# A graph network on one core: first edges of visits by plain transfers, stagings on SyncE, and 14 scatters moved ahead of a run of gathers

## The reference

```
h = relu(layernorm(x))
x = x + gcn(relu(gcn(h)))            # gcn(h) = D^-1/2 (A + I) D^-1/2 h W + b
h = relu(layernorm(x))
msg = relu([h[src], attr] @ W1 + b1)             # one message for each edge
agg = segment_sum(msg, dst) / max(count(dst), 1)
x = x + relu([h, agg] @ W2 + b2)
```

## Time and profile before

| | us |
|---|---|
| median of 3 runs | 2456.9 (2456.45 to 2467.43) |
| the profiled execution, own time | 2462.0 |
| its span | 2460.1 |
| POOL busy | 1822.6 (74%) |
| PE busy | 2155.0 (88%) |
| DVE busy | 1870.1 (76%) |
| ACT busy | 1241.6 (50%) |

### The profile page before, as it was taken

The page is one execution under the profiler, slowest core; times in us unless marked ns, Lnnn a source line. Parts: engine busy times, 40 slices in busy tenths (PEclk is TensorE's granted clock), DMA queues, the critical chain, the costliest instruction groups (busy, mean ns, idle before and its releaser), DMA issues.

```text
span 2460.1 us, 45677 instructions
## 1 busy us (share of the span) xinstructions
PE 2155.0 (88%) x15568; PEld 1771.9 (72%) x15569; DVE 1870.1 (76%) x3574; ACT 1241.6 (50%) x3349; POOL 1822.6 (74%) x1687
## 2 busy tenths in 40 slices
PE   0344899999999998799995599999999999999996
PEld 0133679997667897688884487887787878888885
DVE  6999999998889884544447377777777777777777
ACT  5846246665666773555557243444444434444440
POOL 0867877888888787777777777777777777777770
PEclk9867999999999998999998799999999999999999
DMA  9414233333334351588874243434434343434432
GB/s 359 173 39 140 74 127 127 135 126 126 124 124 163 141 188 45 166 325 302 322 282 149 70 145 103 142 109 121 131 106 145 106 141 109 131 120 118 133 86 60
DMA packets 127247, 358.89 MB, mean 146 GB/s; under 512 B 34082, under 2 KB 77831, under 8 KB 117687
## 3 DMA queue, kind: packets, MB, share of 16 engines
q10 hardware_dynamic: 24752, 186.56, 19.9%
q0 software_dynamic: 56880, 85.25, 13.5%
q1 hardware_dynamic: 45369, 84.00, 9.9%
HBM read 229.75 MB, written 125.93 MB: 145 GB/s over the span
## 4 chain that ended last, share of the span: by engine, by line
PE 52%; POOL 17%; DVE 15%; issue 8%; ACT 4%; DMA 3%; DVEq 1%; POOLq 0%; ACTq 0%; SPq 0%
POOL rows L803 14%; PE ps_feat L1102 6%; PE ps_node L1102 6%; PE ps_node L1117 5%; PE ps_feat L1117 5%; DVE region_c L2079 5%; PE ps_sum L1212 3%; ACT rows L1318 3%; PE pre_banks L1090 3%; PE ps_extra L1250 3%; POOL permuted L821 2%; PE pre_banks L1203 2%; PE ps_feat L1234 2%; PE ps_node L1234 2%; PE ps_sum L1234 2%
## 5 line engine op out<-in xcount | busy, mean ns | idle before, releaser
L821 POOL DMA_INDIRECT permuted<-rows_or_lows,slot_of_edge x768 | 902.5, 1175 | 234.0 <-issue 151.7
L803 POOL DMA_INDIRECT rows<-table,region_a x800 | 786.1, 983 | 243.8 <-issue 236.8
L2079 DVE TENSOR_TENSOR region_c<-iota_key,region_c 128x1568 bf16<-128x1568 f16 (+1 forms) x327 | 355.8, 1088 | 0.0
L1435 ACT ACTIVATE region_a<-pre_banks 128x392 bf16<-128x392 f32 x392 | 195.0, 499 | 146.3 <-PE pre_banks L1090 138.3
L1102 PE MATMUL ps_node<-region_a,region_b 128*128 128x256 bf16 (+1 forms) x1911 | 263.8, 268 | 4.1 <-issue 4.1
L1102 PE MATMUL ps_feat<-region_a,region_b 128*128 128x256 bf16 x1764 | 252.5, 272 | 0.0
L584 DVE CAST wide_counts<-region_a 128x1024 fp32r<-128x1024 bf16 (+2 forms) x163 | 117.2, 723 | 156.4 <-PE ps_node L1117 69.1
L1250 PE MATMUL ps_extra<-msg_parts,target_hot 128*128 128x256 f32 x1176 | 222.7, 305 | 13.8 <-DVE msg_parts L2264 13.6
L582 ACT ACTIVATE wide_counts<-region_a 128x1024 fp32r<-128x1024 bf16 x150 | 158.6, 1060 | 120.7 <-PE ps_node L1117 56.9
L2279 DVE TENSOR_TENSOR target_hot<-consts,region_a 128x512 fp32r<-128x512 f32 x336 | 207.5, 618 | 1.0
L1212 PE MATMUL ps_sum<-onehot,rows 128*128 128x64 f32 x1600 | 202.3, 270 | 0.0
(11 more groups left out here) (319 smaller groups left out, 4790.0 us busy)
## 6 DMA issues: line engine op xcount, KB each, us to landing
counts<-region_a ACTq DMA_DIRECT2D x23, 3136.0 KB
region_a<-counts ACTq DMA_DIRECT2D x11, 3200.0 KB
region_a<-counts ACTq DMA_DIRECT2D x11, 3072.0 KB
rows_or_lows<-block_lows ACTq DMA_DIRECT2D x72, 448.0 KB
permuted<-region_b SPq DMA_DIRECT2D x25, 833.0 KB, 24.4
region_a<-permuted SPq DMA_DIRECT2D x24, 833.0 KB
rows_or_lows<-edge_cols_in POOLq DMA_DIRECT2D x24, 544.0 KB
region_a<-attr_t_in SPq DMA_DIRECT2D x50, 256.0 KB, 2.8
```

Source lines behind the costliest of these rows:

```text
L803: nc.gpsimd.indirect_dma_start(rows[:, s, j * D:(j + 1) * D], None, tables[2], bass.IndirectOffsetOnAxis(ap=message_rows[:, c * TC + j:c * ...
L821: nc.gpsimd.indirect_dma_start(permuted, bass.IndirectOffsetOnAxis(ap=slot_of_edge[:, r * RT + k:r * RT + k + 1], axis=0), edge_rows_of[:, ...
L1435: nc.scalar.activation(counts[strip % 2][:, :, j * W:j * W + W], count_banks[w % BANKS][:, 0:KEYS].rearrange("p (d h) -> p h d", h=SB), AC ...
L2079: v.tensor_tensor(hot_key(u)[:, :, 0:n], iota_key[:, None, 0:n].to_broadcast([P, UNIT // SIDE, n, SIDE]), keys[:, :, None, :].to_broadcast ...
```

## The change

It has four parts.

1. The 21 gathers of starts leave GpSimd. In their place 19 plain transfers (`START_RUNS`) copy from `starts_dram` to a new DRAM array `visit_starts_dram`: a run takes n nodes that lie a fixed step apart and repeats each k times, 4 bytes at a time. SyncE issues ten of them, ScalarE nine, and they copy 2,688 elements (the longest run has 452 x 2). When all have landed SyncE reads the array back into `visit_starts_i` (21 x 128).
2. `find_visits` leaves node phase 0. VectorE waits for that read ahead of node phase 0, shifts and converts the starts, TensorE turns them, and VectorE adds `visit_plan`. TensorE waits for the starts ahead of its first products of node phase 0.
3. GpSimd does 14 scatters of range 0 ahead of its wait for `visit_rows_ready`, and the wait for `blanked` comes before them.
4. SyncE stages ranges 2 to 13, after `store_own(0)`, each when range r-2 has landed; GpSimd stages 0, 1 and 14 to 23.

To keep the number of semaphores, `late_blocks` becomes a `link` (VectorE waits for its own instruction at once) and `late_scanned` is counted on `rank_hot`.

```diff
+def runs_of(parts):
+    runs, visit = [], 0
+    for target, k in parts:
+        if runs and runs[-1][3] == k and (runs[-1][2] == 1 or target - runs[-1][1] == runs[-1][2] * runs[-1][4]):
+            first, at, n, _, step = runs[-1]
+            runs[-1] = (first, at, n + 1, k, step if n > 1 else target - at)
+        else:
+            runs.append((visit, target, 1, k, W))
+        visit += k
+    return runs
+START_RUNS = runs_of(VISIT_TARGETS + [(0, VB * P - sum(VISITS))])
...
+        def spread_starts(engine, run):
+            visit, target, n, k, step = run
+            of = starts_dram[target:target + n * step].rearrange("(n w) a -> n w a", w=step)[:, 0:1].to_broadcast([n, k, 1])
+            engine.dma_start(visit_starts_dram[visit:visit + n * k].rearrange("(n k) a -> n k a", k=k), of,
+                             allow_slow_non_contiguous=True).then_inc(starts_gathered, 16)
+        def stage(engine, r):
+            if r >= 2:
+                engine.wait_ge(scattered[r % 2], (r // 2) * RT * 16)
+            engine.dma_start(edge_rows_of[:, r % 2], ...)
...
 SyncE, behind the read of ends_i:
+            sp.wait_ge(starts_moved, 16)
+            for run in START_RUNS[0::2]:
+                spread_starts(sp, run)
+            sp.wait_ge(starts_gathered, 16 * len(START_RUNS))
+            sp.dma_start(visit_starts_i, visit_starts_dram.rearrange("(b p) a -> b (p a)", p=P)).then_inc(starts_gathered, 16)
 SyncE, behind store_own(0):
+                    for r in range(2, STAGED_BY_SP):
+                        stage(sp, r)
...
 GpSimd:
-            pool.wait_ge(starts_moved, 16)
-            for b in range(VB):
-                nc.gpsimd.indirect_dma_start(visit_start[:, b:b + 1], None, starts_dram, ...).then_inc(starts_gathered, 16)
-            pool.wait_ge(visit_rows_ready, 1)
+            pool.wait_ge(blanked, 16 * (RANGES + 1))
+            scatter(0, end=AHEAD_OF_VISITS)
+            pool.wait_ge(visit_rows_ready, 3)
...
 TensorE, ahead of node phase 0:
+            pe.wait_ge(visit_rows_ready, 1)
+            nc.tensor.transpose(ps_sum[0][:, 0:VB], visit_starts, ident[0:VB, 0:VB]).then_inc(visit_rows_ready, 1)
             pe.wait_ge(rank_taken, EARLY * len(BLOCK_GROUPS))
...
 ScalarE, ahead of its wait for degree_ready:
+            act.wait_ge(starts_moved, 16)
+            for run in START_RUNS[1::2]:
+                spread_starts(act, run)
...
 VectorE:
             ranks_taken(EARLY - 1)
+            dve.wait_ge(starts_gathered, 16 * len(START_RUNS) + 16)
+            link(v.tensor_single_scalar(visit_starts_i, visit_starts_i, 4, ALU.arith_shift_right))
+            v.tensor_copy(visit_starts, visit_starts_i).then_inc(visit_rows_ready, 1)
             (count copied from TensorE's bank)
+            dve.wait_ge(visit_rows_ready, 2)
+            v.tensor_tensor(visit_row[:], ps_sum[0][:, 0:VB], visit_plan[:], ALU.add).then_inc(visit_rows_ready, 1)
...
-                        if n == 0 and g == VISIT_ROWS_AT:
-                            find_visits()
```

More of the change, by code:

```diff
@@ L101 @@
 FIRST_LOWS_AT = (4, 7, 9)
+STAGED_BY_SP = 14
+AHEAD_OF_VISITS = 14
 KEYS = W * SB
@@ L157, in build @@
         tiles_dram = nc.dram_tensor("tiles", (2, NT), I32, kind="Internal").ap()
+        visit_starts_dram = nc.dram_tensor("starts_of_visits", (VB * P, 1), I32, kind="Internal").ap()
         starts_dram = nc.dram_tensor("starts_of_nodes", (NP, 1), I32, kind="Internal").ap()
@@ L240, in build @@
         visit_key_kept = carve(VB)
+        visit_starts_i = carve(P, I32)[0:VB]
+        visit_starts = carve(P)[0:VB]
         used[0] = 0
@@ L437, in build @@
         late_loaded = sem("late_loaded")
-        late_blocks = sem("late_blocks")
-        late_scanned = sem("late_scanned")
+        rows_staged_by_sp = [sem("rows_staged_by_sp_0"), sem("rows_staged_by_sp_1")]
         rows_staged = [sem("rows_staged_0"), sem("rows_staged_1")]
@@ L806, in gather_messages, with scatter @@
                         ).then_inc(e["gathered"][s], 16)
-            def stage(r):
-                pool.dma_start(edge_rows_of[:, r % 2], t["edge_cols"][:, r * RT:(r + 1) * RT].rearrange("p t c -> p (t c)")
-                               ).then_inc(rows_staged[r % 2], 16)
-            def scatter(r, pace=lambda k: None):
+            def scatter(r, pace=lambda k: None, first=0, end=RT):
                 pool.wait_ge(ranked, r + 1)
-                pool.wait_ge(rows_staged[r % 2], 16 * (r // 2 + 1))
-                for k in range(RT):
-                    if k == RT // 2 and 1 <= r < RANGES - 1:
-                        pool.wait_ge(scattered[(r - 1) % 2], ((r - 1) // 2 + 1) * RT * 16)
-                        stage(r + 1)
+                staged(pool, r)
+                for k in range(first, end):
+                    if k == RT // 2 and STAGED_BY_SP <= r + 1 < RANGES:
+                        stage(pool, r + 1)
                     pace(k)
@@ L838, in beside_phase @@
                 pool.wait_ge(G["tab"], group(n, i * NG // (PHASED[n] * RT)) + 1)
-            stage(0)
-            stage(1)
+            stage(pool, 0)
+            stage(pool, 1)
             pool.wait_ge(loaded, 16 * N_LOADS)
@@ L876, in _ @@
                 for r in range(PHASED[n]):
-                    scatter(next(ranges), lambda k: beside_phase(n, r * RT + k))
+                    scatter(next(ranges), lambda k: beside_phase(n, r * RT + k), first=0 if n else AHEAD_OF_VISITS)
                 if n == 0:
@@ L1877, in _ @@
             link(v.reciprocal(degree[:], degree[:]))
-            def find_visits():
-                dve.wait_ge(starts_gathered, 16 * VB)
-                link(v.tensor_single_scalar(visit_start[:], visit_start[:], 4, ALU.arith_shift_right))
-                v.tensor_tensor(visit_row[:], visit_start[:], visit_plan[:, 1], ALU.add).then_inc(visit_rows_ready, 1)
             def scales_of(g):
@@ L2370 @@
     at = ROW * np.arange(EDGE_ROWS)[:, None] + np.arange(P)[None, :]
-    visit_of = np.zeros((3, VB * P), np.int32)
-    parts_of = [(w * W + j * (W // len(splits)), k) for w, splits in zip(WINDOW_AT, SPLITS) for j, k in enumerate(splits)]
-    target_of = np.concatenate([np.full(k, target) for target, k in parts_of])
-    visit_of[0, :sum(VISITS)] = target_of
-    visit_of[1, :sum(VISITS)] = np.concatenate([np.arange(k) for _, k in parts_of]) * (P // ROW)
-    visit_of[2, :sum(VISITS)] = -target_of * SB
-    visit_of = visit_of.reshape(3, VB, P).transpose(2, 0, 1)
+    visit_of = np.zeros((2, VB * P), np.int32)
+    visit_of[0, :sum(VISITS)] = np.concatenate([np.arange(k) for _, k in VISIT_TARGETS]) * (P // ROW)
+    visit_of[1, :sum(VISITS)] = -SB * np.concatenate([np.full(k, target) for target, k in VISIT_TARGETS])
+    visit_of = visit_of.reshape(2, VB, P).transpose(2, 0, 1)
     node_half = P * np.arange(SB)[None, :] + np.arange(P)[:, None] - 0.5
```

27 lines of the change are left out of this document (14 added, 13 removed).

## The result

The changed kernel takes 2475.97 us (median, 2474.68 to 2478.5), the kernel before 2458.18 us beside it on the same chip (2456.45 to 2467.43). The ratio is 1.0066, with a 95% interval of 1.0044 to 1.0089: **slower by 0.7%**, 17.8 us by the medians. The forecast was 2441.1 us. The profiled execution took 2475.01 us; its span is 2473.1, 13.0 us over that of before.

What follows compares the result with a forecast made beforehand. POOL was taken to bound the kernel; -17.3 us (its lateness at the messages) + 1.5 (path) + 0 (stall) = -15.8 us, taking the median from 2456.9 to 2441.1 us. Range 2436 to 2468, the forecast's own 2436 to 2445.

Steps and rivals of the forecast that it cites:

- Stall: 0: At VectorE's new wait ahead of node phase 0: starts back at about 162 to 163, so no stall.
- the starts come so late that the kernel is slower: Rival at VectorE's wait ahead of node phase 0: slower from a stall of 28 us; chance 0.14.
- The elements: In the 19 small transfers: the longest run, 904 elements on one engine at 11.9 ns, takes 10.8 us.
- The rest of the chain: Issues of 0.31 to 0.36 us, last out at about 152; landing about 1.4 us, the read back once more.
- the 3 us to spare: At VectorE's new wait: starts back at about 162 to 163, 3 us spare before any stall.
- POOL's lateness, 17.3 us: At the first gather of messages: POOL starts at 1371.09, the table landed at 1353.8; at most 17.3 us to win.
- The end of the table: Before the messages: the last table transfer, issued at 1351.5, lands 2.3 us later.
- The messages move as a whole: Messages and output groups move with the first chunk, for which VectorE, TensorE and ScalarE stand idle.
- The added path, 1.5 us: On VectorE's path from 166.05 through node phase 0: the added work costs 1.5 us together.
- The 14 scatters: In POOL's idle time from 136.98: 20.7 us, up to 7.5 more beside scans, ending between 158 and 165.
- Part 4, 7 to 11 us: In POOL's scatters: 12 stagings moved to SyncE save 0.6 to 0.9 us each, 7 to 11 us.
- the first gather of messages at about 1355: Sign of a right forecast: POOL's first gather of messages at about 1355 us, after waiting for the last table transfer.

Runs made afterwards that it cites:

- e7: The changed kernel with long runs cut evenly (27 transfers) and the transfers with most elements issued first; 2451.75 us, ratio 0.9966 to the kernel before.
- e10: The changed kernel with GpSimd staging all ranges again, the 14 early scatters kept; 2471.71 us, ratio 1.0046 to the kernel before.
- e8: The changed kernel with GpSimd staging all ranges again and no scatters ahead of the visit edges; 2483.27 us, ratio 1.0079 to the kernel before.
- e1: The changed kernel with every long run cut so its main part is a multiple of 16 (27 transfers); 2455.08 us, ratio 0.998 to the kernel before.
- e9: e6 with ScalarE's first load_lows held until the last table is stored; 2446.22 us, ratio 0.9937 to the kernel before.
- e4: The kernel before with only the stagings of ranges 2 to 13 moved to SyncE, plus small edits; 2458.71 us, ratio 0.999 to the kernel before.
- e5: The kernel before with the small edits and 14 more plain transfers on POOL that nobody reads; 2475.87 us, ratio 1.0063 to the kernel before.
- e6: e1 with VectorE's wait for the starts behind group 1 of node phase 0 and find_visits behind group 2; 2446.3 us, ratio 0.9945 to the kernel before.
- e3: The changed kernel with POOL's gathers of starts and find_visits in node phase 0 kept, 8 scatters ahead; 2447.66 us, ratio 0.9959 to the kernel before.
- e12: e3 with three more scatters before the visit_row wait and ScalarE's first load_lows held until the table is stored; 2445.5 us, ratio 0.9928.

## Why the prediction was wrong

The step that failed is **"Stall: 0"**. VectorE waited 27.5 us, and everything up to the table moved by it. I had seen the place: the price was bounded there from 155 to 183.5 us for the start of the rest (stall 0 to 17.5, or 50 by a doubled price), and the rival that the starts come so late that the kernel is slower, with a chance of 0.14, named VectorE's wait and a stall of 28 us as its point of no return. At 27.5 us that rival is, all but its last half us, what happened.

By the traces the first gather of messages was to come at 1355.3 us (1371.09 - 17.3 + 1.5) and came at 1384.24, 28.9 us later. This is the stall (+27.5), the landing of the last table transfer (5.2 us and not 2.3, +2.9) and the 0.95 us from there to the gather, less the earlier end of the ranks (-0.7), the shorter added path (-0.4) and 1.3 us that the stages between node phase 0 and the table gave back. Read point by point:

- **The elements.** I took 904 elements on one engine at 11.9 ns, 10.8 us. The fullest engine has 847 by the cut. That the numbers are near each other is luck: the run of 904 lies on four engines, 226 on each, and the 847 are the sum over many runs, 382 of them from the run of 191. The price was wrong: 29.6 ns from 171.1 to 190.2 us over 646 elements. The term is 25 us and not 10.8. The row that it came from the earlier trace rows was of another kind, and I read packets as if they were elements. The 21 gathers of 2,688 starts are 672 packets (from 148.3 to 187.5 us of the kernel before):

```profile
q0 software_dynamic: 672, 0.01, 1.3%
```

  That is 32 for each gather of 128 elements; by the packet records 16 of them have 32 bytes, which is eight elements, and 16 have 4 bytes. In the new transfers each element is a packet of its own. Also those gathers read DRAM and write SBUF, one transfer at a time, while here DRAM is the target and two queues stand behind each other; what makes a tenth of the packets so slow, no run separates. With even cuts and the largest runs first only 18 of 3,007 took over 20 ns (e7), so the slow ones go with the uneven cut more than with the 4 bytes. I had written that a doubled price wasn't excluded, and then took the low end.
- **The rest of the chain.** Issue at 0.31 to 0.36 us each, last out at 152: measured 0.7 us each, and the last blocked until 177.3. By the line through the three kernels some 17 us up to the read back don't depend on the fullest engine (148 to 165), and the read back takes 2.7 more (190.18 to 192.89), where I had 3 to 4 for both. The two terms are short by 14 and 16 us; that is the stall of 27.5 and the 3 us to spare that went with it. In these 17 us lie the 5 to 8 us without a packet ahead of the last landing and about 4 us by which the 14 scatters hold up the transfers (e10 against e8). e1 shows that this second term is enough for a stall: 201 elements on the fullest engine are 6 us, and 7.8 us of stall are left.
- **POOL's lateness, 17.3 us.** It was 14.7: the table's last landing was read from the median, 2.3 us, where it took 4.0, and 0.95 us to the gather were left out. What there was has been won in full, since POOL waits for the table in the changed kernel.
- **The end of the table.** In the changed kernel it was 6.1 us from last issue to first gather. Two transfers of the lows, freed by the earlier scatters, met it where one had before. I had costed the early scatters as pure gain and not asked what else they release and hold up. e9 shows that a hold shortens the landing; that it is worth time isn't shown.
- **The messages move as a whole.** Right: 1088.9 against 1089.0 us. Over the twelve kernels that ran this stage took between 1083 and 1092 us, which is the accuracy of that term.
- **The added path, 1.5 us.** 1.1. (The `link` in it was written as at most 0.5 us; 14 times 0.05 would be 0.7. No run shows it by itself.)
- **The 14 scatters.** 20.7 us and up to 7.5 more were forecast; 24.9 measured, 1.78 each. Their worth: from e8 to e10 they bring the last scatter 24.5 us forward, 1.75 each. But in the changed kernel they only fill an idle time that part 1 makes: with parts 3 and 4 left out POOL waits 54.6 us for `visit_row`.
- **Part 4, 7 to 11 us.** 5.1 from e10 to the changed kernel, where nothing else differs, and 0 in e4 against the kernel before, while 14 issues added cost 14.7. The number of scatters begun by a given time, counted in the traces:

```
us                 240   600   760   960  1080  1320
before              13   248   333   466   555   728
stagings alone e4   13   251   335   467   554   727
14 more        e5   13   245   325   456   543   717
part 4 out     e10  23   258   344   467   555   729
changed             24   263   350   473   560   733
```

e4 gains three scatters by 600 us and has all but one of them lost by 960, between the end of the strips and node phase 1, where single scatters take longer (1140 ns on average from 770 to 1060, before 1114). e5, in which POOL stages, has 1130 there, so SyncE's stagings aren't the only thing that may lengthen them. Why taking away doesn't give what adding takes is open: the small edits that e4 and e5 share and the kernel before hasn't are an untested rival.

With the stall away the result is close to the forecast of 2441.1 us, a ratio of 0.9936, and "the first gather of messages at about 1355": e6 has 1356.34 and 0.9945 (0.9931 to 0.9958). It isn't the same kernel (even cuts, the wait inside node phase 0), and it waits for the table as forecast, 12.5 us, with the 5.1 us of landing that the forecast didn't have.

## What to carry to other kernels

A wait that is moved from an engine with slack to the one that sets the path is a bet on the slowest landing, not on the bytes (here 11 KB in 19 transfers took 43 us); put such a wait at the last place where its result is still in time (even cuts take 0.7% slower to 0.2% faster, the wait two groups later to 0.55% faster), and let an engine with idle time keep the work if that costs nobody (e3, with the gathers left on POOL and its idle time filled, has 0.9959, and the interval overlaps with that of e6). When a price is taken from a row, ask whether that row has the same bytes in a packet, the same target, the same number of queues and the same cut. When a time is taken from a median, ask whether the one transfer that is waited for is like the others. Where an engine gets early, ask what its semaphores release.

## What the runs showed of the hardware

- 4-byte elements from DRAM to DRAM: one packet each, and one more for each engine that a transfer is cut over (1,010 + 69 = 1,079 packets on ScalarE's queue). The wait grows by 27 to 33 ns for each element on the fullest of the engines. A packet took 44 ns on average in the changed kernel, but 9 in the median, and 11.6 on average in e7; in the gathers to SBUF it was 11.9 ns, with eight elements in every second packet.
- An issue of such a transfer takes SyncE or ScalarE 0.6 to 0.8 us, not 0.31. Where one engine holds a long backlog, a later issue on the same queue blocks its engine: 12.7 and 23.3 us, gone with even cuts (0.8 and 1.4 us at most).
- Behind the last issue of small elements it took 13.8 us (e1) and 11.1 us (e7) until all had landed, though the backlog of the fullest engine was 201 elements. The last 8.0 and 5.4 us of it, and 6.9 in the changed kernel, come after the last packet. What fills them stays open.
- Scatters of POOL beside such transfers hold them up: 42.2 us from first issue to read back with 14 scatters (e10), 38.1 without (e8), in one execution each.
- A 256 KB table transfer lands in 2.3 us with no transfer of the lows beside it (e9, e12), in 4.0 when one 448 KB transfer went out 0.9 us ahead of it (before), in 5.1 and 5.2 with two out 0.8 to 1.2 us ahead (e6, changed kernel), and in 3.6 with two out about 2 us ahead (e1).
- A plain transfer that POOL issues among its scatters takes it 0.6 us. All in all 14 of them moved its last scatter by 14.7 us (e5), and 12 taken away by 5.1 (e10 to the changed kernel).
